# A pre-norm transformer block on one Trainium2 core: the tokens of batches 2 and 3 split in place and transposed by DMA instead of by TensorE

## What is computed

```python
B, S, D, HIDDEN = 4, 1024, 128, 384
x = x + attention(layernorm(x), W_qk, W_v, alibi_slope)
x = x + ffn(layernorm(x), w_gate, w_up, w_down)

def attention(x):                       # one head, causal
    scores = (x @ W_qk) @ x.T / sqrt(D) + (kpos - qpos) * slope
    return softmax(where(qpos >= kpos, scores, -inf)) @ (x @ W_v.T)

def ffn(x):                             # integer weights / 127
    return (silu(x @ wg.T) * (x @ wu.T)) @ wd.T
```

## Time and profile before

| | us |
|---|---|
| median of 3 runs | 143.63 (143.48 to 143.95) |
| the profiled execution's own time | 143.12 |
| its span in the trace | 141.1 |
| busy: PE / DVE / ACT / POOL | 119.1 / 119.3 / 109.4 / 103.4 |
| attention of the four batches ends at (last L832 of each) | 42.8, 63.9, 83.9, 103.0 |

### The profile page before, as it was taken

How to read it: one execution, slowest core, us unless ns; L and a number is a source line. 1 busy time by engine, 2 the same in 40 slices (tenths; PEclk the granted TensorE clock), 3 DMA queues, 4 the chain that set the end, 5 groups by cost and what they waited for, 6 DMA issues and landing times.

```text
span 141.1 us, 3405 instructions
## 1 busy us (share of the span) xinstructions
PE 119.1 (84%) x1183; PEld 88.1 (62%) x1183; DVE 119.3 (85%) x336; ACT 109.4 (78%) x249; POOL 103.4 (73%) x162
## 2 busy tenths in 40 slices
PE   0278578999999999889999998988994789979961
PEld 0066164768987869777869975667842545656661
DVE  0759989998788995989987969998869999998892
ACT  4035779999966999757999949977869689988920
POOL 6491789964992545996895999479669999995810
PEclk9999999999999999999999999999999999999999
DMA  4896000000000000000000001643001303057625
GB/s 133 230 255 177 3 2 2 5 2 0 5 0 0 5 0 2 0 5 0 0 5 0 5 0 40 99 89 79 0 5 37 79 0 79 6 73 213 198 78 153
DMA packets 18515, 7.28 MB, mean 52 GB/s; under 512 B 9152, under 2 KB 18496, under 8 KB 18496
## 3 DMA queue, kind: packets, MB, share of 16 engines
q1 hardware_dynamic: 18496, 7.02, 20.6%
HBM read 2.82 MB, written 2.10 MB: 35 GB/s over the span
## 4 chain that ended last, share of the span: by engine, by line
PE 32%; DVE 27%; POOL 14%; ACT 13%; DMA 5%; issue 5%; SPq 2%; DVEq 0%; POOLq 0%
DVE probsT_lo L805 5%; POOL hidden_lo L411 5%; PE work_ps L553 5%; PE attn_ps L566 3%; DVE biased L822 3%; DVE stats L707 3%; PE score_ps L501 3%; PE score_ps L503 3%; DMA x2T_lo<-xn_lo 3%; PE attn_ps L568 3%; PE attn_ps L567 3%; PE score_ps L502 3%; ACT probs L960 3%; ACT probsT_hi L982 2%; DVE xs L832 2%
## 5 line engine op out<-in xcount | busy, mean ns | idle before, releaser
L566 PE MATMUL attn_ps<-v_hi,probsT_hi 128*128 128x128 f16 x144 | 25.8, 219 | 2.4 <-DVE xs L832 1.7
L805 DVE TENSOR_TENSOR probsT_lo<-work_ps,probsT_hi 128x512 f16<-128x512 f32 (+3 forms) x48 | 25.2, 553 | 3.0 <-ACT probsT_hi L982 2.7
L960 ACT ACTIVATE probs<-biased,neg_max 128x128 f32<-128x128 f32 (+7 forms) x32 | 25.0, 783 | 3.2 <-DVE neg_max L822 3.1
L982 ACT CAST probsT_hi<-work_ps 128x512 f16<-128x512 f32 (+3 forms) x48 | 21.4, 483 | 6.4 <-PE work_ps L553 6.2
L822 DVE CUSTOM_DVE_ANT_0 biased<-score_ps,bias,neg_score_scale 128x128 f32<-128x128 f32 (+7 forms) x32 | 25.8, 806 | 0.6 <-PE score_ps L503 0.6
L568 PE MATMUL attn_ps<-v_hi,probsT_lo 128*128 128x128 f16 x144 | 25.8, 219 | 0.0
L567 PE MATMUL attn_ps<-v_lo,probsT_hi 128*128 128x128 f16 x144 | 25.7, 219 | 0.0
L553 PE MATMUL work_ps<-ident,probs 128*128 128x128 f32 x144 | 21.4, 274 | 1.3 <-DVE probsT_lo L805 0.7
L707 DVE BATCH_NORM_STATS2 stats<-xs 128x6 f32<-128x128 f32 x64 | 15.2, 283 | 5.2 <-DMA xs<-in_L_attn_x_dram 3.7
L553 PEld LDWEIGHTS work_ps<-ident,probs 128*128 128x128 f32 x144 | 16.5, 141 | 4.4 <-DVE probsT_lo L805 1.0
L566 PEld LDWEIGHTS attn_ps<-v_hi,probsT_hi 128*128 128x128 f16 x144 | 14.1, 98 | 5.5 <-DVE probsT_lo L805 1.8
(11 more groups left out here) (138 smaller groups left out, 331.5 us busy)
## 6 DMA issues: line engine op xcount, KB each, us to landing
out_dram<-xs SPq DMA_DIRECT2D x7, 256.0 KB, 3.2
xs<-in_L_attn_x_dram SPq DMA_DIRECT2D x3, 512.0 KB, 8.2
xs<-in_L_attn_x_dram SPq DMA_DIRECT2D x2, 256.0 KB, 3.1
out_dram<-xs SPq DMA_DIRECT2D x2, 128.0 KB, 2.0
wgu_int<-in_L_ffn_w_gate_dram SPq DMA_DIRECT2D x1, 192.0 KB, 3.0
wgu_int<-in_L_ffn_w_up_dram SPq DMA_DIRECT2D x1, 192.0 KB, 3.1
wd_int<-in_L_ffn_w_down_dram SPq DMA_DIRECT2D x1, 192.0 KB, 3.5
x2T_hi<-xn_hi SPq DMA_TRANSPOSE x8, 2.5
```

The costliest lines, as they stand in the source:

```text
L566: pe.matmul(attn_ps[:, 0:D], p_hi, v_j, start=(j == 0), stop=False)
L805: dve.tensor_tensor(probsT_lo[:, i % 2, cols], work_ps[:, bank, 0:n], probsT_hi[:, i % 2, cols], ALU.subtract).then_inc(work_emptied, 1)
L960: act.activation(probs[:, i % 2, 0:n], biased[:, i % 2, 0:n], ACT.Exp, bias=neg_max[:, i:i + 1], scale=-1.0, accum_out=prob_sum[:, i:i + 1 ...
L982: act.copy(probsT_hi[:, i % 2, CW * h:CW * h + n], work_ps[:, bank, 0:n]).then_inc(probsT_hi_ready, 1)
```

## The change

Batches 2 and 3 get their xT from DMA. The parts xT0 and xT1 are taken out of the streams of PE, ACT and POOL and out of the ring at batches 1 and 2. Instead ACT casts `xn` of rounds 2 and 3 to `xn_hi`, POOL makes `xn_lo`, and SP issues eight more DMA transposes, straight into `xT_hi` and `xT_lo`. SP waits until all scores of batch n-2 are made before the first transpose of round n, because `xT` has two buffers. PE's q0 and q1 parts wait for the landing.

The casts are placed by `tokens_at`: those of round b+2 beside tiles 6 and 7 of batch b, for b = 0, 1, 2; those of round 5 beside tiles 1 and 2 of batch 3. So the casts of round 4 move from tiles 0 and 1 of batch 3 to tiles 6 and 7 of batch 2, and those of round 5 move one tile earlier.

POOL's order is new as well: `moments` of the following round stands ahead of the q splits of batches 1 and 2; the `token_low` of rounds 2, 3 and 4 stand behind their `scale`, and so those of round 4 stand ahead of the norm of round 5.

`stats` gets a third buffer for round 4, so that the statistics of round 4 no longer wait for POOL.

```diff
--- before.py
+++ after.py
@@ -56,10 +56,12 @@
     NROUND = 2 * B
+    BY_DMA = 2
     def parts_at(b, i):
-        return prologue[i - 1:i] if i and b < B - 1 else []
+        parts = prologue[i - 1:i] if i and b < B - 1 else []
+        return [part for part in parts if part[0] != "xT" or b + 1 < BY_DMA]
     ring = [(kind, 0, h) for kind, h in prologue] + [("P", 0, 0, 0)]
@@ -81,6 +83,10 @@
     def by_pool(key):
         return key[0] in ("xT", "q") and key[1] > 0
+
+    def copied_high(key):
+
+        return sum(k[0] != "P" for k in ring[:ring_index[key] + 1])
     def emptied(key):
@@ -144,7 +150,7 @@
         xs = sb("xs", [P, NT, D], F32)
-        stats = sb("stats", [P, 2, TB, 6], F32)
+        stats = sb("stats", [P, 3, TB, 6], F32)
         mean_sum = sb("mean_sum", [P, TB], F32)
         mean_dif = sb("mean_dif", [P, TB], F32)
         dif_sq = sb("dif_sq", [P, TB], F32)
@@ -244,7 +250,7 @@
         attn_added = sem("attn_added")
         xn_hi_ready = sem("xn_hi_ready")
         xn_lo_ready = sem("xn_lo_ready")
-        x2T_landed = [[sem(f"x2T_landed{par}{h}") for h in range(HALVES)] for par in range(2)]
+        tokens_landed = [[sem(f"tokens_landed{par}{h}") for h in range(HALVES)] for par in range(2)]
         gate_up_ready = sem("gate_up_ready")
         silu_ready = sem("silu_ready")
         hidden_ready = sem("hidden_ready")
@@ -263,6 +269,10 @@
             return int(n in (0, B + 3))
+        def stats_of(n):
+
+            return 2 if n == B else apart(n)
+
         def steps_before(n):
             return N_STEPS * n - 1 if n else 0
@@ -272,10 +282,10 @@
         def split_before(n, h):
-            return HALVES * (n - B) + h
+            return HALVES * (n - BY_DMA) + h
         def landed(n):
-            return 32 * ((n - B) // 2 + 1)
+            return 32 * ((n - BY_DMA) // 2 + 1)
         def pool_blocks(c):
             return 0 if c == 0 else 1 if c in (1, NCH - 1) else HB - 1
@@ -302,14 +312,18 @@
               .then_inc(slope_loaded, 16)
             for b in range(1, B):
                 sp.dma_start(xs[:, TB * b:TB * (b + 1), :], xv[b]).then_inc(x_loaded[b], 16)
-            for n in range(B, NROUND):
+            for n in range(BY_DMA, NROUND):
+                if n < B:
+
+                    sp.wait_ge(scores_ready, TB * (n - 1))
                 for h in range(HALVES):
                     tiles = slice(CT * h, CT * (h + 1))
-                    for part, ready, o in ((xn_hi, xn_hi_ready, x2T_hi), (xn_lo, xn_lo_ready, x2T_lo)):
+                    for part, ready, xT, x2T in ((xn_hi, xn_hi_ready, xT_hi, x2T_hi), (xn_lo, xn_lo_ready, xT_lo, x2T_lo)):
+                        o = x2T[:, HALVES * (n - B) + h, :] if n >= B else at(xT, n % 2, slice(CW * h, CW * (h + 1)))
                         sp.wait_ge(ready, split_before(n, h) + 1)
-                        sp.dma_start_transpose(o[:, HALVES * (n - B) + h, :].rearrange("p (t q) -> p t q", q=P),
+                        sp.dma_start_transpose(o.rearrange("p (t q) -> p t q", q=P),
                                                part[:, n % 2, tiles, :].rearrange("p t d -> p (t d)"))\
-                          .then_inc(x2T_landed[n % 2][h], 16)
+                          .then_inc(tokens_landed[n % 2][h], 16)
             for c in range(NCH - 1):
                 sp.wait_ge(result_ready, c + 1)
                 sp.dma_start(ov[:, CT * c:CT * (c + 1), :], xs[:, CT * c:CT * (c + 1), :]).then_inc(stored, 16)
@@ -348,7 +362,7 @@
             def moments(n):
-                steps, stat = steps_before(n), stats[:, apart(n), :, :]
+                steps, stat = steps_before(n), stats[:, stats_of(n), :, :]
                 half, quarter, per_element, eps, power = (norm_const[:, k:k + 1].broadcast_to([P, TB]) for k in range(5))
                 def small(out, a, b, op):
@@ -383,7 +397,7 @@
             def scale(n):
-                if n >= B + 2:
+                if n >= BY_DMA + 2:
                     pool.wait_ge(xn_lo_ready, split_before(n - 1, 0))
                 elif n >= 2:
                     pool.wait_ge(work_filled, filled(("xT", n - 2, HALVES - 1)))
@@ -440,19 +454,23 @@
                 for h in range(HALVES):
                     split_low(b, b % 2, kind, h)
+            split_lows(1, "xT")
             for b in range(1, B - 1):
-                split_lows(b, "xT")
+                moments(b + 1)
                 split_lows(b, "q")
-                norm(b + 1)
+                centre(b + 1)
+                scale(b + 1)
+                for h in range(HALVES):
+                    token_low(b + 1, h)
             moments(B)
-            split_lows(B - 1, "xT")
             centre(B)
             split_lows(B - 1, "q")
             scale(B)
+            for h in range(HALVES):
+                token_low(B, h)
             norm(B + 1)
-            for n in (B, B + 1):
-                for h in range(HALVES):
-                    token_low(n, h)
+            for h in range(HALVES):
+                token_low(B + 1, h)
             norm(B + 2)
             moments(B + 3)
             token_low(B + 2, 0)
@@ -525,8 +543,10 @@
                         pe.wait_ge(first_half_ready, 1)
                     else:
                         pe.wait_ge(xn_ready, HALVES * b + h)
+                elif b < BY_DMA:
+                    taken(("xT", b, h))
                 else:
-                    taken(("xT", b, h))
+                    pe.wait_ge(tokens_landed[b % 2][h], landed(b))
                 fill((kind, b, h), {"xT": transpose_x, "q": project_q, "v": project_v}[kind])
             def scores(b, par, i):
@@ -579,7 +599,7 @@
                 def product(with_lo):
                     n, h = B + c // HALVES, c % HALVES
-                    pe.wait_ge(x2T_landed[n % 2][h], landed(n))
+                    pe.wait_ge(tokens_landed[n % 2][h], landed(n))
                     for j in blocks:
                         if c:
                             pe.wait_ge(hidden_ready, HB * (c - 1) + j + 1)
@@ -700,11 +720,11 @@
             def statistics(n, j):
-                if j == 0 and n not in (0, 1, B + 3):
-                    dve.wait_ge(pool_step, steps_before(n) - N_STEPS + N_READ)
+                if j == 0 and n not in (0, 1, B, B + 3):
+                    dve.wait_ge(pool_step, steps_before(n - 1 if n == B + 1 else n) - N_STEPS + N_READ)
                 if j == 0 and B <= n < B + 3:
                     dve.wait_ge(attn_added, TB * (n - B + 1))
-                m = dve.bn_stats(stats[:, apart(n), j, :], at(xs, TB * (n % B) + j, slice(0, D)))
+                m = dve.bn_stats(stats[:, stats_of(n), j, :], at(xs, TB * (n % B) + j, slice(0, D)))
                 if j == TB - 1:
                     m.then_inc(stats_done, 1)
@@ -790,7 +810,7 @@
                 bank = bank_of((kind, b, h))
                 hi, lo = {"xT": (xT_hi, xT_lo), "q": (qT_hi, qT_lo), "v": (v_hi, v_lo)}[kind]
-                dve.wait_ge(hi_ready, len(prologue) * b + prologue.index((kind, h)) + 1)
+                dve.wait_ge(hi_ready, copied_high((kind, b, h)))
                 cols = slice(CW * h, CW * h + CW)
                 dve.tensor_tensor(at(lo, par, cols), work_ps[:, bank, :], at(hi, par, cols), ALU.subtract)\
                    .then_inc(work_emptied, 1)
@@ -963,9 +983,14 @@
             def token_high(n, h):
                 tiles = slice(CT * h, CT * (h + 1))
                 act.wait_ge(xn_ready, HALVES * n + h)
-                if n >= B + 2:
-                    act.wait_ge(x2T_landed[n % 2][h], landed(n - 2))
+                if n >= BY_DMA + 2:
+                    act.wait_ge(tokens_landed[n % 2][h], landed(n - 2))
                 act.copy(xn_hi[:, n % 2, tiles, :], xn[:, n % 2, tiles, :]).then_inc(xn_hi_ready, 1)
+
+            def tokens_at(b, i):
+
+                at_tiles = {(b + 2, 0): TB - 2, (b + 2, 1): TB - 1} if b < B - 1 else {(B + 1, 0): 1, (B + 1, 1): 2}
+                return [part for part, tile in at_tiles.items() if tile == i]
             def scale_sum(b, i):
@@ -997,8 +1022,8 @@
                         copy_probsT(b + 1, 0)
                     for part in parts_at(b, i):
                         copy_high(b + 1, nxt, *part)
-                    if final and i < 2 * HALVES:
-                        token_high(B + i // HALVES, i % HALVES)
+                    for n, h in tokens_at(b, i):
+                        token_high(n, h)
             act.wait_ge(const_ready, N_CONST)
```

## The result

The changed kernel takes 152.63 us (median of 4 runs, 152.15 to 153.37) against 143.56 us before (4 runs): a ratio of 1.063, 95% interval 1.058 to 1.068. The profiled execution took 153.37 us, of which its span is 151.4.

A forecast was written before the change was run, and what follows sets the result against it. No busy share alone named the bound: PE, DVE and ACT ran in step, POOL mattered by when it delivers. +2.3 + 1.3 - 1.2 + 3.6 = +6.0 us on 143.12, plus 0.5 for the median, gave 149.6 us; range 146.0 to 151.6.

The forecast's parts named there:

- The moved moments: Batches 0 and 1: POOL's moments ahead of q make PE wait 2.55 and 2.6 us; +2.3 and +1.3 us.
- The moved casts: Batch 3: xn of round 5 comes late, ACT's tile 2 is 4.1 us late; +3.6 us, bounds 2.5 and 4.3.
- Rival (a): TensorE's clock falls to half at batch 3's wait, 2.3 us more per tile: 152 to 154 us; chance 0.10.
- the forecast's own signs of being wrong: Low half of q0 starting before moments end, ACT reaching round 5's cast after its xn, or PE's granted clock below 1.00.
- The level at the start: Clock at 2.4 GHz in all 40 slices, yet transposes at the start took 430 ns against 274 later, the lower level.
- The gain of batch 2: Batch 2: transposes taken from PE and ACT save 1.2 us, between 0.8 (DVE's tile 5 wait alone) and 2.0.
- The third buffer: Batch 1: removes DVE's 1.51 us wait for POOL, but the gain goes into the wait for q0.
- The sum: Whole kernel: +2.3 + 1.3 - 1.2 + 3.6 = +6.0 us on the profiled execution's 143.12 us.
- half way: Whole kernel: 147.9 to 151.2 us around 149.6, from the terms' bounds taken together half way.
- The DMAs: Eight added transposes land in 2.5 us, 4.4 at worst, with over 5 us of cover; costed at nothing.
- The rest of the kernel: Behind batch 3: later steps shift with batch 3's statistics, so the feed-forward part keeps its length.

The follow-up runs named there:

- experiment 2: Changed kernel with POOL's order at batches 1 and 2 as before (both low halves of q, then the whole norm of the following round): 147.69 us, ratio 1.025.
- Experiment 1: Changed kernel with 20 useless transposes of the identity ahead of each of PE's three long waits, the waits for data kept: 149.75 us, ratio 1.042.
- experiment 9: Kernel of experiment 6, with ACT casting tile 6's transposed probabilities ahead of tile 7's exponentials at tile 5 of batches 0 to 2: 142.58 us, ratio 0.989.
- experiment 5: Kernel before the change with the third statistics buffer and nothing else of the change: 143.05 us, ratio 0.995.
- Experiment 7: Changed kernel, POOL's orders restored, casts beside tiles 0 and 1 of the next batch, moments of round 4 ahead of round 3's token_low: 143.89 us, ratio 1.001.
- experiments 6: Changed kernel, both POOL orders as before, casts moved to tile 7 and next batch's tile 0, round 5's to tiles 2 and 3: 141.61 us, ratio 0.983.
- experiments 4: Changed kernel with both of POOL's orders (at the q parts and around the norm of round 5) as before: 143.5 us, ratio 1.000.

## Why the prediction was wrong, point by point

The direction, the places and the sizes of the waits were right; the time lay 3.0 us above the forecast and 1.0 above the range. The step that failed is the price of PE's waits: it had their length and nothing for the clock.

- **The moved moments.** Forecast: PE late by 2.55 and 2.6 us, batches 0 and 1 longer by 2.3 and 1.3. Measured: waits of 2.42 and 2.78 us, and with the clock up 2.06 and 1.12 us. Right.
- **The moved casts.** Forecast: ACT's tile 2 late by 4.1 us, batch 3 longer by 3.6. Measured: a wait of 4.10 us, and with the clock up 3.4. Right. ACT stood ready for this cast 2.73 us after the last add of batch 2, and before the change the cast there started 2.84 us after it, so the wait is almost all lateness of `xn`.
- **The clock: the step that failed.** Rival (a) had the mechanism, but a chance of 0.10 and only batch 3 for its place. I reasoned that 1.89 us of idle PE had not lost the clock and left 2.4 to 2.8 us without a price, though a clock below 1.00 was among the forecast's own signs of being wrong. The runs showed a loss after each of the three waits, 1.7, 1.6 and 1.3 us in the trace (0.7 for the third in the trace of experiment 2). Experiment 1 isolates it: keep PE busy, and the median is 149.75 for a forecast of 149.6. The Trainium skill, "TensorE: Matmul & The Clock Gate", section "Why this matters for your kernels", says that a PE left idle between bursts goes back to half clock; the trace agrees, with rests of 2.42, 2.78 and 2.29 us. The right reading would have been that a wait longer than the longest in the trace of before has an unknown price in the clock, with nothing and a tile at half clock as its ends, at each place.
- **The level at the start.** The prediction has the clock up in all 40 slices and, two sentences on, transposes at the lower level at the start. Both are read from the trace of before, and they don't agree: the six transposes of the earlier trace rows at 8.6 to 9.7 us took 421 ns (one 474) although the row says 1.00 there. In the trace after, the same form took 421 ns at a granted clock of 0.50 (104.3 to 105.4 us) and 273 at 1.00. So the durations speak for the lower level, and the clock row is not to be trusted that early.
- **The gain of batch 2.** Forecast 1.2 us, from DVE's wait of 0.84 us in tile 5 and small ones. Measured 0.55, all in tiles 2 to 4 (2.24, 2.57 and 3.14 us for 2.46, 2.76 and 3.27). The wait did not move, in the DVE timeline after:

```profile
84.01 1.16 DVE L825 TENSOR_TENSOR probsT_lo<-work_ps,probsT_hi 128x512 f16<-128x512 f32 x2 [0.84 <-ACT probsT_hi L1007]
```

ACT saved its copies in tiles 1 and 2, where it then waited for DVE's maxima and for PE; nothing of it is left by tile 5, where ACT's own steps seem to bind (experiment 9). The 0.65 us too much is a mis-sized term.

- **The third buffer.** I priced it at 1.1 us where nothing covers it, and said that the wait for q0 would swallow it. Alone it is 0.6 to 0.7 (experiment 5). In the changed kernel it gave nothing, as predicted.
- **The sum.** With the clock up the steps measured +2.06, +1.12, -0.55 and +3.40, together +6.03 for the forecast's +6.0. That close a sum is partly luck: three terms were 0.2 us too high each, and the gain of batch 2 was 0.65 too high as well. By my estimate the whole 9.1 us are these 6.0, some 4.0 for the clock and 1.1 less behind batch 3, to within 0.2. The prediction's range "half way" between its bounds is 147.8 to 151.0 by plain halves, not 147.9 to 151.2; nothing hangs on it.
- **The DMAs.** Costed at nothing, and nothing it was: no wait of PE for landing tokens. Experiment 7 shows the edge of that cover.
- **The rest of the kernel.** I had it keep its length; in the trace it was 1.1 us shorter, by a landing that is told of below.

## What to carry to other kernels

In an in-order engine's stream, look at what each instruction waits for before looking at what it costs: ten small instructions, 3.5 us in all, that wait for the last statistics delay everything behind them, and the part that has been ready for some time, here q0, belongs ahead of them. A stall that the trace of before does not hold should be priced twice on TensorE, once for its length and once for the matmuls that follow at half clock; when a kernel has idle stretches as long as those here (2.3 to 2.8 us), a few transposes of no use in them tell the two apart in one run. And a change that saves 1 to 2 us by giving three engines less to do can lose 9 by the order in which a fourth delivers: with two moves in POOL's list the same change is 1.7% faster than the kernel before. And a gain is best read by the stage: of the 2.6 us or so that this is, only 1.5 lie in the stage that was changed.

## What the runs showed of the hardware that I had not expected

- The clock fell after PE had started again, not while it was idle. PE resumed at 37.26 us after 2.42 us of rest, and the window from 37 to 38 us is still granted in full; the window from 38 to 39 has 0.55. It stayed low for some 3.4 us in batches 0 and 1, and for 6.8 us in batch 3. In experiment 2, after the same rest in batch 3 and with PE about as busy behind it (0.6 and 0.4 of the first two windows), it was 3.4 us. What sets the length was not tried.
- The rest alone does not decide. The 1.89 us in the feed-forward part had no such effect in any trace, nor had rests of 2.2 us near the end of the traces of experiments 6 and 9, which stop some 4 us later. Of the four executions of experiment 2, three have a mean clock of 0.988 and one, the fastest, 0.997. And one or two executions each of experiments 4, 6, 7 and 9, whose traces show no lower clock, have 0.982 to 0.989, against 0.997 or more in all executions of the kernel before; no trace was kept of them.
- One DMA transpose of most traces takes over 2 us to issue instead of 1.2 to 1.3. In five of the eleven traces it is the third of round 4; in four it is another, and in two there is none. In the SP timeline of the changed kernel, and of experiment 1:

```profile
90.45 2.43 SPq L324 DMA_TRANSPOSE x2T_hi<-xn_hi  x1
...
134.79 1.27 SPq L324 DMA_TRANSPOSE x2T_hi<-xn_hi  x1
```

```profile
130.12 2.23 SPq L324 DMA_TRANSPOSE x2T_hi<-xn_hi  x1
```

In the changed kernel it fell on round 4, where nobody waits. In the kernel before, the SP timeline and the waits near the end show:

```profile
122.15 1.19 SPq L310 DMA_TRANSPOSE x2T_lo<-xn_lo  x1
123.38 2.14 SPq L310 DMA_TRANSPOSE x2T_hi<-xn_hi  x1
...
PE score_ps L587 <- DMA x2T_lo<-xn_lo: 1.0, 1, 1.0
```

PE waited 1.0 us, but not for the transpose that was long to issue: it waited for the one issued at 122.15, which landed after 4.0 us, where the same one of the changed kernel landed after 2.4. Experiment 1 is like the kernel before. Experiment 5 has the landing after 4.2 us and PE's wait of 1.1 us with no long issue in that round:

```profile
122.62 1.19 SPq L314 DMA_TRANSPOSE x2T_lo<-xn_lo  x1
123.86 1.27 SPq L314 DMA_TRANSPOSE x2T_hi<-xn_hi  x1
...
PE score_ps L591 <- DMA x2T_lo<-xn_lo: 1.1, 1, 1.1
```

The late landing accounts for 1.0 of the 1.1 us by which the rest behind batch 3 differed. What causes it, or the long issue, was not tried, and one trace per kernel does not tell whether it goes with the kernel or with the execution.
